# A decoder layer on one Trainium2 core: attention denominators in four column groups, their inverses spread through memory, and VectorE's order of work changed

## The reference, cut to what matters

```python
q = elu(x @ Wq) + 1 ; k = elu(x @ Wk) + 1 ; v = x @ Wv      # 16 heads of 64
a = sigmoid(x @ Wa + ba + 2.0)                              # one decay per head and token
# token by token:
S = a * S + k (outer) v ;  z = a * z + k
out = (q . S) / (q . z + 1e-6)                              # num / den, den one number per head and token
y = out @ Wo ;  x1 = layernorm(x + y)
```

## Time and profile before

| | |
|---|---|
| median of 3 runs | 1417.74 us (1414.22 to 1418.28) |
| the profiled execution | 1417.32 us |
| its span in the trace | 1415.5 us |
| mean granted clock of TensorE | 0.954 |
| busy: PE, PEld, DVE, ACT, POOL | 1281.5, 1079.2, 832.9, 948.9, 738.9 us |

### The profile page before, as it was taken

One profiled execution on the slowest core, in us unless ns is written; L12 is line 12 of the kernel. 1 busy time (PEld: TensorE's weight loads), 2 busy tenths in 40 slices (PEclk: granted clock), 3 DMA queues, 4 the chain that ended last, 5 costly groups with the idle time before them and its releaser, 6 DMA issues. The chain is left out here.

```text
span 1415.5 us, 30098 instructions
## 1 busy us (share of the span) xinstructions
PE 1281.5 (91%) x10053; PEld 1079.2 (76%) x10053; DVE 832.9 (59%) x1643; ACT 948.9 (67%) x2118; POOL 738.9 (52%) x837
## 2 busy tenths in 40 slices
PE   5999999999999999999889999954599999998780
PEld 5788888888888888888667777743488888888780
DVE  4444555544555544455558888847466666666564
ACT  4777777777777777777747777754466666665453
POOL 1344444444444444444557777720467777776653
PEclk9999999999999999999989999975699999999895
DMA  4333222222222222222133443323356666666637
GB/s 164 91 105 85 77 91 69 83 68 76 76 87 67 84 66 76 78 79 71 53 118 82 117 109 100 88 75 96 116 131 161 158 161 158 157 160 148 182 67 245
DMA packets 155791, 151.30 MB, mean 107 GB/s; under 512 B 48882, under 2 KB 124250, under 8 KB 155674
## 3 DMA queue, kind: packets, MB, share of 16 engines
q1 hardware_dynamic: 140698, 129.18, 30.0%
q0 software_dynamic: 14976, 20.62, 8.1%
HBM read 113.45 MB, written 33.84 MB: 104 GB/s over the span
## 5 line engine op out<-in xcount | busy, mean ns | idle before, releaser
L569 DVE TENSOR_TENSOR a_probs<-a_ps_s,a_decay 128x384 f32<-128x384 f32 x256 | 134.9, 553 | 160.5 <-PE a_ps_o L736 121.6
L367 POOL TENSOR_SCALAR_AFFINE_SELECT a_decay<-a_decay 128x256 f32<-128x256 f32 x256 | 110.6, 435 | 224.5 <-ACT a_decay L447 224.5
L376 POOL TENSOR_TENSOR a_key_sum<-a_probs 128x256 f32<-128x256 f32 x128 | 97.4, 761 | 157.8 <-DVE a_probs L569 157.8
L1854 POOL DMA_INDIRECT sum_rows<-e_y_out,e_target x78 | 126.1, 1617 | 81.0 <-ACT e_y_out L1908 54.2
L420 ACT ACTIVATE a_qk_exp<-a_ps_qk 128x512 f32<-128x512 f32 x124 | 74.2, 598 | 124.9 <-PE a_ps_qk L664 124.5
L562 DVE SCALAR_TENSOR_TENSOR a_qk<-a_qk_exp,a_qk_relu 128x512 f32<-128x512 f32 x128 | 91.2, 713 | 111.6 <-ACT a_qk_relu L421 111.6
L664 PE MATMUL a_ps_qk<-a_xT_hi,a_w_hi 128*128 128x256 f32 x496 | 139.2, 281 | 1.1 <-DVE a_xT_lo L537 1.1
L664 PE MATMUL a_ps_qk<-a_xT_lo,a_w_hi 128*128 128x256 f32 x496 | 138.6, 280 | 0.0
L664 PE MATMUL a_ps_qk<-a_xT_hi,a_w_lo 128*128 128x256 f32 x496 | 138.6, 279 | 0.0
L445 ACT ACTIVATE a_decay<-a_c_rows,a_c_col 128x256 f32<-128x256 f32 x256 | 129.6, 506 | 0.0
L1835 POOL DMA_INDIRECT e_x_in<-x_rows,e_index x78 | 80.3, 1030 | 79.5 <-DVE e_index L2000 56.4
(11 more groups left out here) (306 smaller groups left out, 3902.9 us busy)
## 6 DMA issues: line engine op xcount, KB each, us to landing
a_c_rows<-a_c_scratch SPq DMA_DIRECT2D x128, 256.0 KB, 3.2
e_gu_raw<-in_L_ffn_gate_w SPq DMA_DIRECT2D x23, 512.0 KB
e_gu_raw<-in_L_ffn_up_w SPq DMA_DIRECT2D x23, 512.0 KB
e_dn_raw<-in_L_ffn_down_w SPq DMA_DIRECT2D x23, 512.0 KB, 5.4
a_x_in<-in_x SPq DMA_DIRECT2D x16, 256.0 KB
a_x_res<-in_x SPq DMA_DIRECT2D x16, 256.0 KB, 2.7
x_rows<-a_x SPq DMA_DIRECT2D x16, 256.0 KB, 3.3
x_bo_rows<-a_x_bo SPq DMA_DIRECT2D x16, 256.0 KB, 3.9
```

The source lines that it names most:

```text
L367: pool.affine_select(out=d, in_=d, compare_op=ALU.is_ge, fill=0.0, base=0, pattern=[[0, 2], [1, P]], channel_multiplier=-1)\
L376: pool.tensor_tensor(key_sum[:], probs[:, :, P:N], probs[:, :, N:TRI], ALU.add).then_inc(keys_summed, 1)
L569: vec.tensor_tensor(probs[:, h, :], ps_s[h][:, 0:TRI], decay[h][:], ALU.mult)\
L1854: pool.indirect_dma_start(sum_dram, bass.IndirectOffsetOnAxis(target[par][:, blk:blk + 1], 0), y_out[par][:, blk, :], None, compute_op=ALU ...
```

## The change

`ones` becomes 128x32. The four denominator matmuls of a pair (head 0 early and late queries, head 1 early and late queries) go to four groups of 32 columns of the array and to four groups of 32 output partitions, so that 128 columns of PSUM hold all of them. ScalarE takes logarithm and exponent of 128x128 instead of 128x256. The inverses then lie in the wrong partitions: SyncE stores four rows (one from each group) in memory (`store_den`), waits for that, and loads them back over 64 partitions for each head (`spread_den`, two loads of 64 partitions by 256 floats). `normalise` waits for those loads. SyncE's list is rewritten around this, and `c_rows` is fetched four pairs ahead instead of three. ScalarE inverts before it copies `oT_hi`. VectorE does `weigh`, then `finish_qk` (in slot 0 `finish_qk` still comes first), then `normalise`. The buffer `z_exp` goes; `z_sb` is overwritten in place.

```diff
@@ SyncE
+            def store_den(n):
+                sp.wait_ge(rden_done, n + 1)
+                sp.dma_start(rden_dram[n % 4], rden_row[n % 2][0:P:DENS, :]).then_inc(rden_stored, 16)
+
+            def spread_den(n):
+                sp.wait_ge(rden_stored, 16 * (n + 1))
+                if n >= 2:
+                    sp.wait_ge(oT_done, n - 1)
+                for h in range(2):
+                    row = rden_dram[n % 4, 2 * h:2 * h + 2, :].rearrange("(a t) i -> a (t i)", a=1)
+                    sp.dma_start(rden[n % 2][h * DH:(h + 1) * DH, :], row.to_broadcast([DH, N])).then_inc(rden_spread[n % 2], 16)
...
+                    n = b * PAIRS + g
+                    store_den(n)
+                    if g == 4 and b + 1 < B:
+                        store_c(b + 1)
+                    if g == 5 and b + 1 < B:
+                        spread_c(n + ROWS_AHEAD - 1)
+                    if g != 4 and n + ROWS_AHEAD < B * PAIRS:
+                        spread_c(n + ROWS_AHEAD)
+                    spread_den(n)
+                    if g == 0 and b + 2 < B:
+                        load_x(b + 2)
...
@@ ScalarE
                 act.wait_ge(o_made, n + 1)
-                act.activation(ln_den[:], ps_o[g % 2][:, 1, :], ACT.Ln, bias=den_eps[:]).then_inc(ln_done, 1)
+                act.wait_ge(rden_done, n)
+                act.activation(ln_den[:], ps_o[g % 2][:, 1, 0:P], ACT.Ln, bias=den_eps[:]).then_inc(ln_done, 1)
                 act.wait_ge(ln_done, n + 1)
                 if exists(b, g, 2):
-                    act.wait_ge(oT_done, n - 1)
-                act.activation(rden[g % 2][:], ln_den[:], ACT.Exp, scale=-1.0).then_inc(rden_done, 1)
+                    act.wait_ge(rden_stored, 16 * (n - 1))
+                act.activation(rden_row[g % 2][:], ln_den[:], ACT.Exp, scale=-1.0).then_inc(rden_done, 1)
...
+                    if exists(b, g, 1):
+                        before, _, pair = back(b, par, g, 1)
+                        invert_den(before, pair)
                     if exists(b, g, 2):
                         before, _, pair = back(b, par, g, 2)
                         high_oT(before, pair)
-                    if exists(b, g, 1):
-                        before, _, pair = back(b, par, g, 1)
-                        invert_den(before, pair)
@@ VectorE
             def normalise(b, g):
                 n = b * PAIRS + g
-                vec.wait_ge(rden_done, n + 1)
+                vec.wait_ge(rden_spread[g % 2], 32 * (n // 2 + 1))
...
+                    if g == 0:
+                        finish_qk(*projected_before(b, g))
+                    weigh(b, g)
+                    if g and has(b, 1):
+                        finish_qk(*projected_before(b, g))
                     if exists(b, g, 2):
                         before, _, pair = back(b, par, g, 2)
                         normalise(before, pair)
-                    if g == 0 or has(b, 1):
-                        finish_qk(*projected_before(b, g))
-                    weigh(b, g)
@@ TensorE
-                for h in range(2):
-                    pe.matmul(out[h][:, 1, 0:P], ones[:], probs[:, h, 0:P], start=True, stop=True)
+                dens = [ps_o[g % 2][t * DENS:(t + 1) * DENS, 1, 0:P] for t in range(4)]
                 pe.wait_ge(keys_summed, n + 1)
                 for h in range(2):
-                    mm = pe.matmul(out[h][:, 1, P:N], ones[:], key_sum[:, h, :], start=True, stop=True)
+                    pe.matmul(dens[2 * h], ones[:], probs[:, h, 0:P], start=True, stop=True, tile_position=(0, 2 * h * DENS))
+                    mm = pe.matmul(dens[2 * h + 1], ones[:], key_sum[:, h, :], start=True, stop=True,
+                                   tile_position=(0, (2 * h + 1) * DENS))
```

More of the change, by code:

```diff
@@ L157, in linear_attention @@
     ROWS_AHEAD = 4
+    DENS = P // 4
     DECAY_SHIFT, EPS, Z_FLOOR = 2.0, 1e-6, -80.0
@@ L178, in linear_attention @@
         ident = cross.ident
-        ones, scan_ones = sb("a_ones", [P, DH]), sb("a_scan_ones", [H, N])
+        ones, scan_ones = sb("a_ones", [P, DENS]), sb("a_scan_ones", [H, N])
         x_in, x_res = sb("a_x_in", [P, NB, D]), sb("a_x_res", [P, NB, D])
         xT_hi, xT_lo = sb("a_xT_hi", [P, KC, N], F32R), sb("a_xT_lo", [P, KC, N], F32R)
-        z_sb, z_exp, decT = sb("a_z", [H, N]), sb("a_z_exp", [H, N]), sb("a_decT", [H, N])
+        z_sb, decT = sb("a_z", [H, N]), sb("a_decT", [H, N])
         cT = sb("a_cT", [H, N])
@@ L193, in linear_attention @@
         probs, key_sum = sb("a_probs", [P, 2, TRI]), sb("a_key_sum", [P, 2, P])
-        ln_den, rden = sb("a_ln_den", [P, N]), [sb(f"a_rden{n}", [P, N]) for n in range(2)]
+        ln_den, rden_row = sb("a_ln_den", [P, P]), [sb(f"a_rden_row{n}", [P, P]) for n in range(2)]
+        rden = [sb(f"a_rden{n}", [P, N]) for n in range(2)]
+        rden_dram = nc.dram_tensor("a_rden_scratch", [4, 4, P], F32).ap()
         oT = [sb(f"a_oT{n}", [P, N]) for n in range(2)]
@@ L224, in linear_attention @@
         c_turned, c_kept = sem("a_c_turned"), sem("a_c_kept")
+        rden_stored, rden_spread = sem("a_rden_stored"), [sem(f"a_rden_spread{n}") for n in range(2)]
         rows_loaded = [sem(f"a_rows_loaded{n}") for n in range(ROWS_AHEAD)]
@@ L315, in sequence @@
                 for g in range(PAIRS):
-                    ahead = b * PAIRS + g + ROWS_AHEAD - 1
-                    if g and ahead < B * PAIRS:
-                        spread_c(ahead // PAIRS, ahead % PAIRS)
-                    if g == 0:
-                        if b + 2 < B:
-                            load_x(b + 2)
-                        if ahead < B * PAIRS:
-                            spread_c(ahead // PAIRS, ahead % PAIRS)
+                    n = b * PAIRS + g
[9 more added lines that the diff above has]
+                        load_x(b + 2)
                     if g == 1 and b < cross.LOAD_PARTS:
@@ L327, in sequence @@
                         load_residual(b)
-                    if g == 4 and b + 1 < B:
-                        store_c(b + 1)
                     if g == 6 and b >= 1:
@@ L338, in _ @@
             store_c(0)
-            for g in range(ROWS_AHEAD - 1):
-                spread_c(0, g)
+            for n in range(ROWS_AHEAD):
+                spread_c(n)
             for b in range(B):
@@ L510, in _ @@
             all_sequences(act, sequence)
+            invert_den(B - 1, PAIRS - 1)
             high_oT(B - 1, PAIRS - 2)
-            invert_den(B - 1, PAIRS - 1)
             high_oT(B - 1, PAIRS - 1)
```

9 lines of the change are left out of this document (5 added, 4 removed).

## The result

Three timed rounds beside the kernel before, on one chip:

| | before | after |
|---|---|---|
| median of 4 runs | 1415.98 us | 1451.49 us |
| lowest to highest | 1413.30 to 1418.28 | 1449.38 to 1453.49 |
| ratio, 95% interval | | 1.0246 (1.0229 to 1.0264) |
| profiled execution, its span | 1417.3, 1415.5 | 1450.13, 1448.4 |
| mean granted TensorE clock | 0.954 | 0.954 |

The account below looks back on a forecast made before the run. TensorE was taken to bound the kernel, with a new VectorE-ScalarE ring of 4.90 us overtaking it. Full sequences +9.2, last sequence +1 and stage end +3.6 made +13.8 us: 1431 from 1417.3, range 1412 to 1460.

Parts of the forecast that it names:

- the ring: Exp, decays, masks, `weigh`, `finish_qk`, `normalise`, `high_oT`, exp wait in a circle: 4.90 us, +9.2 us over fifteen sequences.
- T 22.94 + 4.99: Slot 0 in the sum over a sequence: TensorE starts at 22.94, takes 4.99, ends at 27.93 us.
- TensorE's gain, 0.06: Denominator matmuls per slot: 0.22 saved less 0.16 for the change of tile shape, ends 0.01 and 0.22.
- the forecast's 0.22: Four denominator matmuls in four column groups should take 0.22 us instead of 0.44.
- Hidden by 1 us, at no cost: Inverses' way through memory in sequences with projections: 4.4 us, under a cover of 5.4 to 6.0.
- never waits for a DMA before the last sequence: Sign that the forecast is right: `normalise` has no DMA wait until the last sequence.
- nothing: SyncE's queue: waits longer, but load_x, residual loads and x1 stores have a slot or more of lead; no cost.
- the end, +4.6: Memory path uncovered: last sequence +1 us, end of the stage after its last `normalise` +3.6 us.
- The ring is hidden: Rival: the ring is 4.3 us or less, TensorE stays the bound; 1415 us, the same; chance 0.15.
- the faster one: Rival: besides a hidden ring, changing from 64 to 32 columns costs nothing; 1396 us; chance 0.12.
- VectorE and GpSimd collide: Rival: `finish_qk` beside `key_sum` is stretched, ring 5.05 to 5.6; 1442 to 1480 us; chance 0.17.
- Memory is late: Rival: memory way takes 6.4 us, `normalise` waits, slots 5.1 each; +14 and +6, 1451 us; chance 0.11.

Follow-up runs that it names:

- experiment 1: Kernel before with only the two new orders on VectorE and ScalarE, old denominators, nothing through memory: 1434.5 us, ratio 1.0137.
- Experiment 5: Kernel after with `normalise` between `weigh` and `finish_qk` on VectorE, memory path kept: 1435.8 us, ratio 1.0147 to the kernel before.
- experiment 11: Kernel before with VectorE's new order alone, ScalarE still copying `oT_hi` before it inverts: 1516.65 us, ratio 1.0671.
- experiment 4: Kernel after with ScalarE's rounding of x's high part ahead of the `oT_hi` copy in slot 7: 1441.71 us, ratio 1.0188 to the kernel before.
- experiment 2: Kernel before with only the denominators in four column groups, no memory path, late queries' inverses in wrong partitions: 1402.75 us, ratio 0.9908.
- Experiment 12: Kernel after with `normalise` before `finish_qk`, one `c_rows` load a slot, cross-attention loads one a slot: 1429.15 us, ratio 1.0060 to the kernel before.
- experiment 7: Kernel after with SyncE issuing the `c_rows` load behind the two spreads instead of ahead: 1456.32 us, ratio 1.0292 to the kernel before.
- Experiment 6: Kernel after with the last sequence's denominators and inverses made as before, nothing stored or spread: 1441.74 us, ratio 1.0193 to the kernel before.
- experiment 3: Kernel after with ScalarE's `oT_hi` copy behind the exp and relu of the projection: 1443.16 us, ratio 1.0202 to the kernel before.

## Why the prediction was right in sign and wrong in size

The time lies in the range, but in a part that the range held open for a collision and for memory that is late in every slot. Neither set the time, so that it lies there is luck.

**Right: the ring.** The new bound was to be 4.90 us in slots 6 and 7. It is 4.89, hop by hop, and experiment 1 shows it without the rest of the change. Slots 3 and 4 were to stay TensorE's, slot 5 nearly, and they are. Experiment 5 takes `finish_qk` out of it and the ring is gone; experiment 11 puts 0.8 us more in and it grows by that.

**Wrong term 1: slot 0, "T 22.94 + 4.99".** The forecast let ScalarE's copy of x delay the decays (the 0.48) but had TensorE's projection start freely. It needs x's low part, which hangs on the same late copy. The slot is 5.79 us instead of 5.38; the wait adds 0.41 a sequence, about 6 us, and experiment 4, which moves the copy out of the ring as well, wins 8. This is a missed waiter: the forecast followed the instruction into the decays and not into its second reader.

**Wrong term 2: TensorE's gain, 0.06.** It measured 0.12 (experiment 2). If four groups at a time save the forecast's 0.22, which is an estimate, the change from 64 to 32 columns costs 0.22 - 0.12 = 0.10 us net and not 0.16. By itself this is 7 us in the good direction. In the kernel after it shows in the slots that TensorE sets, where they are 0.28 a sequence shorter than forecast, and term 1 outweighs it. The Trainium skill, TensorEngine Tiling (Array Packing), Key Properties, says that a change of mode drains the engine: the trace has a gap there (0.17), but the net price by this estimate is half of the 0.21 that I had read off the change back to 128 columns.

**Wrong term 3: "Hidden by 1 us, at no cost".** The way was put at 4.4 us and is 4.85 with nothing in front. The cover of 5.4 to 6.0 would still do, and in sequences 9 to 14 it does but for one wait of 0.27 us. In sequences 0 to 8 it doesn't, for 8.4 us, against the sign "never waits for a DMA before the last sequence". The forecast said of SyncE's queue "nothing", having asked only whether the large loads would be late. What suffers is the small transfer among them: a way of two dependent transfers, each able to wait behind a 256 KB one. Experiment 12 shows the part of the burst for sequence 0, and experiment 7 that of neighbouring transfers. In sequences 3 to 8 it is nearly always pair 5, behind two `c_rows` loads. Why these land later there than from sequence 9 on, behind the same two loads, stays open.

**Wrong term 4: the end, +4.6.** It was +12.7. The last seven slots have no projection to cover the way (+4.7, of which experiment 1 puts 1.0 down to the order), and the last pair pays 7.64 us for it, behind x1's stores. Experiment 6 wins back 8.1 of these 12.7 in its trace (1.7 and 6.4).

**The rivals.** *The ring is hidden* and *the faster one* are excluded by the ring's own 4.89. *VectorE and GpSimd collide*: `finish_qk` kept its 0.68, and it is `key_sum` that stretches, as the lines of the two kernels show (duration ns min/median/max; before, then after):

```profile
L376 POOL TENSOR_TENSOR a_key_sum<-a_probs x104: 725/738/953, 81.2 to 627.0; 128x256 f32<-128x256 f32 x104
```

```profile
L395 POOL TENSOR_TENSOR a_key_sum<-a_probs x100: 723/1012/1026, 80.2 to 623.4; 128x256 f32<-128x256 f32 x100
```

The median is 0.27 us longer, and nobody on the ring waits for it. In experiment 5 `key_sum` starts first, beside `normalise` (one input in PSUM), and its median is back at 0.73; `finish_qk`, started 0.09 behind it, takes 1.20 instead of 0.68. The Trainium skill, SBUF — State Buffer, SBUF: two separate sides, lets the one that starts first keep the port, and both orders agree in who waits. So the rival's collision is real, and the ring was spared it because `finish_qk` starts 0.26 us ahead of `key_sum` (547.26 and 547.52), as the forecast had argued. *Memory is late* gave 1451, the time measured, but by another road: it had `normalise` wait for memory in every slot, and it waits 8 times in the windows read. Its price for the end (+6) was the nearest to the truth.

## What to carry to other kernels

When a step moves behind another on an in-order engine, write down every reader of every instruction that the new ring makes late, not only the next one in the ring: here x's split (slot 0) was worth 0.67 us a sequence (5.79 to 5.12 in experiment 4) and, in experiment 3, the low part of `oT` some 1.6 (43.0 against the 41.41 of experiment 2), where the ring itself takes 0.98 in slots 5 to 7. A value sent through memory on a deadline of one slot must be costed as a chain of transfers in the queue in which it really stands, in the fullest stretch and in the stretch without cover, not in the typical one. And an order is cheap to repair: with `normalise` ahead of `finish_qk` and the inverses spread within SBUF, and with the `c_rows` and cross-attention loads one a slot and the last sequence kept out of it, the same idea goes from 2.5% slower to 0.5% faster.

## What the runs showed of the hardware that I had not expected

- Going from 64-column to 32-column tiles with all 128 rows shows a gap of 0.17 us. The four denominators gain 0.12 a slot in all, so by the estimate above the change costs 0.10 net, half of what the way back to the full array shows.
- A 2 KB store that completes in 1.6 us when no large load is close takes 2.0 to 3.3 in many slots of experiment 7, where one to three 256 KB transfers were issued up to 2 us before it on the same queue, and 3.7 to 4.6 behind a burst (kernel after, sequences 1 and 0).
- A 64 KB load that spreads one row of HBM over 64 partitions occupies SyncE for 0.55 us and lands 2.7 after its issue. A 32 KB spread within SBUF occupies it for 0.62 and lands 1.9 after.
- GpSimd's addition of two SBUF inputs takes 1.01 us instead of 0.74 when VectorE's `finish_qk` started just before it. When the addition started first, it is `finish_qk` that takes 1.20 instead of 0.68 (experiment 5).
